# Softmax denominators of a transformer block: five of sixteen tiles a head summed by accumulating DMA

## The chip, the core and the metric

The kernel runs on one core of a Trainium2 chip. The metric is the device time of one execution in microseconds (us). The engines are PE (TensorE), DVE (VectorE), ACT (ScalarE), POOL (GpSimd) and SP (SyncE, which here only issues DMAs). Each runs its own instructions in order and waits for the others by semaphores. The core has 16 DMA engines; a DMA can be issued by SP, ACT or POOL.

## The reference, cut to what matters

A transformer block with adaptive norms: B=2 sequences, L=2048 rows, D=512, H=16 heads of 32, a hidden width of 1024.

```
shift_msa, scale_msa, gate_msa, shift_mlp, scale_mlp, gate_mlp = split(silu(c) @ Wada + bada, 6)
h = _ln(x) * (1 + scale_msa) + shift_msa
q, k, v = h @ Wq + bq, h @ Wk + bk, h @ Wv + bv        # 16 heads each
A = softmax(q @ k.T / sqrt(32))                         # 2048 x 2048 for each of 32 (batch, head) pairs
x = x + gate_msa * ((A @ v) @ Wo + bo)
h2 = _ln(x) * (1 + scale_mlp) + shift_mlp
out = x + gate_mlp * (gelu(h2 @ W1 + b1) @ W2 + b2)
```

## The kernel before, in words

Three stages follow one another. The first computes the modulation, the norm and q, k, v in eight chunks of 512 rows. The second is attention: 32 heads (`g`, G = 32), each in 16 steps (`t`, NT = 16), one step for each tile of 128 keys against all 2048 queries. The third projects, and runs the MLP in eight chunks. Large products are made of a rounded high part and a low remainder ("hi" and "lo"), three matmuls for one.

In step `t` of head `g` PE computes the scores of tile `t` in four parts of 512 queries (L1338, L1340, L1342 and the subtraction of the row maximum, L1347), 16 matmuls; between them four "maximum" matmuls (L1326) of the next head, which DVE reduces (L1055); then `values`, the product of v with the exponentials of tile `t-1` (L1360). ACT turns each score bank into exponentials (L844), four to a tile, in `prob`, a ring of RING = 4 tiles: the exponentials of tile `t` overwrite those of tile `t-4`, so ACT waits first until the last reader of tile `t-4` is done (in `probs`).

The denominator of the softmax is the sum of the exponentials over all 2048 keys. It is collected in two ways. Tiles 0, 1, 3, 4, 6, 7, 9, 10, 12 and 13 (POOL_TILES) are added up by POOL in `psum_acc`, in halves of 1024 columns, nine adds a head and half (`sum_probs`, L695). Their sum, and each of the tiles 2, 5, 8, 11, 14 and 15 (PE_TILES), are summed over the partitions by a group of four matmuls with ones (`sums_of`, L1351), each tile's group one step after its scores, the group of POOL's sum at step 1 of the next head. ACT copies each group's bank (L822) and issues a DMA of the row to DRAM (L824). SP reads the 7 rows of a head back (`load_sums`), DVE adds them and takes the reciprocal at step 8 of the next head (`denominators`).

POOL may start a head's adds only when the group over its last sum is done (`den_mm`), since `psum_acc` is used again.

Seven PSUM banks are given out by a table made in advance (`bank_table`), which takes for each use the bank that should be free first; PE waits in `bank_free` for the former user of that bank, an exponential, a maximum or a copy of sums. The table decides which wait stands where.

The weights wo and w1 (12 pieces of 128 x 512, `late`) are loaded and split during heads 0 to 5, two pieces a head, at steps 4 and 11: ACT writes the high part (L804), DVE the low part (`split_late_lo`, L1087) between its maximum reduces.

`gate` and `gate_b` hold the two gates on all partitions; `gate` is written in the first stage and next read in head 31 (`residual1`, L1115).

## Time and profile before

| what | us |
|---|---|
| median of 3 runs | 2526.02 (2525.95 to 2527.97) |
| the profiled execution | 2520.45 |
| its span in the trace | 2518.7 |
| PE busy | 2405.8 (96%) |
| DVE busy | 1757.6 (70%) |
| POOL busy | 1506.6 (60%) |
| ACT busy | 1421.9 (56%) |

The profiled execution is one run of its own; what lies around its span is 1.75 us. The attention stage runs from about 360 us to about 2050 us. Busy shares are means over three stages with different limits, so the part of the attention that repeats (from 732 us on) is read by itself. In the rows below a line number such as L1351 is the line of the kernel above, an idle time in square brackets stands before the first instruction of its row and names what ended it, and a row with x8 merges eight instructions.

### The profile page before, as it was taken

Reading aid. Unit: us, or ns where it says so; the run is one execution under the profiler, and the core shown is the slowest. Engines: PE = TensorE matmul, PEld = TensorE weight load, DVE = VectorE, ACT = ScalarE, POOL = GpSimd, SP = SyncE. Lnnn points to the kernel's source line nnn. Section 1 sums busy time; section 2 is a strip of 40 time slices with the busy share of each in tenths; the row PEclk is TensorE's granted clock in tenths of the full one; section 3 lists DMA queues with packets and bytes.
Section 4 is the critical chain, followed back from the end, with each engine's and each line's share of the span. In section 5 each row is a group of like instructions: output and inputs, shape, how many; then the busy total and the mean of one; then the engine's idle time right before and its main releaser. Section 6 shows DMA issues by size and latency. Waiting matters only on the chain.

```text
span 2518.7 us, 49885 instructions
## 1 busy us (share of the span) xinstructions
PE 2405.8 (96%) x19544; PEld 1356.3 (54%) x19544; DVE 1757.6 (70%) x2878; ACT 1421.9 (56%) x2622; POOL 1506.6 (60%) x706
## 2 busy tenths in 40 slices
PE   7999889988899999999999999999999888999998
PEld 5788653433344444444444444444444347888887
DVE  5444567777778888888888888888888326566563
ACT  3233225666677777777777777777777542222221
POOL 0000116777688788878887888888788634332320
PEclk9999988999999999999999999999999889999999
DMA  8655561332222332233223322332332111332200
GB/s 273 212 172 187 150 172 35 76 69 62 62 54 54 79 80 54 58 75 80 54 60 79 75 54 67 80 66 54 79 80 50 49 57 50 101 82 67 67 34 34
DMA packets 212631, 210.39 MB, mean 84 GB/s; under 512 B 120064, under 2 KB 152832, under 8 KB 203008
## 3 DMA queue, kind: packets, MB, share of 16 engines
q1 hardware_dynamic: 209904, 205.59, 31.5%
q8 instruction: 143, 2.34, 0.4%
q10 hardware_dynamic: 2512, 1.86, 0.3%
q14 instruction: 72, 0.59, 0.1%
HBM read 146.30 MB, written 60.82 MB: 82 GB/s over the span
## 4 chain that ended last, share of the span: by engine, by line
PE 86%; DVE 4%; ACT 3%; DMA 2%; issue 2%; POOL 1%; SPq 1%; ACTq 0%; POOLq 0%
PE ps L1360 19%; PE ps L1229 19%; PE ps L1326 10%; PE ps L1338 9%; PE ps L1351 8%; PE ps L1469 7%; PE ps L1340 6%; PE ps L1342 4%; PE ps L1347 3%; ACT work L844 1%; DVE weights_r L1087 1%; DVE part_max L1055 1%; POOL work L695 1%; PE ps L1238 1%; ACT work L822 1%
## 5 line engine op out<-in xcount | busy, mean ns | idle before, releaser
L695 POOL TENSOR_TENSOR work<-work 128x1024 f32<-128x1024 f32 x576 | 1355.1, 2409 | 384.7 <-PE ps L1351 227.2
L1055 DVE TENSOR_REDUCE part_max<-ps 128x1 f32<-128x512 f32 x1984 | 1232.1, 682 | 306.6 <-PE ps L1326 306.6
L844 ACT ACTIVATE work<-ps 128x512 f32<-128x512 f32 x2048 | 1058.9, 602 | 382.0 <-PE ps L1347 355.8
L1360 PE MATMUL ps<-work 128*32 128x512 f32 x4096 | 556.8, 616 | 0.2 <-ACT work L844 0.2
L1326 PE MATMUL ps<-acts_r 32*128 32x512 f32 x1344 | 420.5, 478 | 26.1 <-DVE part_max L1055 23.9
L1229 PE MATMUL ps<-acts_r,weights_r 128*128 128x512 f32 x1536 | 381.9, 399 | 4.9 <-DVE acts_r L975 3.9
L1229 PEld LDWEIGHTS ps<-acts_r,weights_r 128*128 128x128 f32 x1536 | 292.2, 192 | 69.8 <-issue 6.8
L1338 PEld LDWEIGHTS ps<-acts_r 32*128 32x128 f32 x1408 | 146.5, 186 | 323.2 <-DVE part_max L1055 172.4
L1338 PE MATMUL ps<-acts_r 32*128 32x512 f32 x1408 | 299.5, 474 | 16.5 <-ACT work L844 7.9
L1340 PE MATMUL ps<-acts_r 32*128 32x512 f32 x1408 | 259.3, 398 | 0.0
L1326 PEld LDWEIGHTS ps<-acts_r 32*128 32x128 f32 x1344 | 182.0, 185 | 137.7 <-DVE part_max L1055 121.7
L1351 PE MATMUL ps<-work,ones 128*32 128x512 f32 x1792 | 242.1, 613 | 0.0
L1347 PE MATMUL ps<-acts_r,minus_r 1*128 1x512 f32 x1024 | 230.6, 446 | 0.2 <-DMA acts_r<-max_T 0.2
L1347 PE MATMUL ps<-m_odd,minus_r 1*128 1x512 f32 x1024 | 228.2, 442 | 0.0
L897 ACT ACTIVATE work<-ps,b_sb 128x512 f32<-128x512 f32 x64 | 44.0, 690 | 307.7 <-PE ps L1229 307.7
L1326 PE MATMUL ps<-acts_r,w_r 32*128 32x512 f32 x640 | 200.7, 474 | 14.2 <-DVE part_max L1055 13.2
L1229 PE MATMUL ps<-weights_r,acts_r 128*128 128x512 f32 x768 | 186.2, 396 | 12.4 <-DVE acts_r L1105 9.4
L668 POOL TENSOR_TENSOR var_eps<-var_eps,mv 128x4 f32<-128x4 f32 x16 | 3.2, 203 | 316.1 <-DVE mv L953 316.1
L710 POOL TENSOR_TENSOR work<-work,gate_b 128x512 f32<-128x512 f32 x60 | 86.1, 1467 | 169.8 <-DMA work<-in_x 149.4
L1342 PE MATMUL ps<-acts_r 32*128 32x512 f32 x1024 | 186.3, 397 | 0.0
L1342 PE MATMUL ps<-w_r,acts_r 32*128 32x512 f32 x1024 | 185.5, 396 | 0.0
L1469 PE MATMUL ps<-w_r,acts_r 128*128 128x512 f32 x768 | 184.4, 391 | 0.0
(88 smaller groups left out, 2553.7 us busy)
## 6 DMA issues: line engine op xcount, KB each, us to landing
acts_r<-k_hi SPq DMA_DIRECT2D x130, 256.0 KB, 4.7
acts_r<-k_lo SPq DMA_DIRECT2D x129, 256.0 KB, 4.8
work<-in_x SPq DMA_DIRECT2D x16, 1024.0 KB, 5.3
q_hi<-work SPq DMA_DIRECT2D x32, 256.0 KB, 2.6
q_lo<-work SPq DMA_DIRECT2D x32, 256.0 KB, 3.3
k_hi<-work SPq DMA_DIRECT2D x32, 256.0 KB, 2.5
k_lo<-work SPq DMA_DIRECT2D x32, 256.0 KB, 3.2
v_rows<-work SPq DMA_DIRECT2D x32, 256.0 KB, 2.0
```

The lines of the kernel that those rows point to most:

```text
L695: nc.gpsimd.tensor_tensor(psum_acc[:, at], first, prob[:, t % RING, at], ALU.add).then_inc(add_ok, 1)
L844: nc.scalar.activation(prob[:, t % RING, j * CH:(j + 1) * CH], ps[:, bank, :], ACT.Exp, scale=SCALE).then_inc(exp_ok, 1)
L1055: nc.vector.tensor_reduce(part_max[:, r * TT + q // NQ, q % NQ:q % NQ + 1], ps[:, bank, :], AX.X, ALU.max).then_inc(a_max, 1)
L1229: mm = nc.tensor.matmul(o, lhs(s, kk), rhs(r, kk), start=(kk == 0 and s == r), stop=(kk == KC - 1 and s == 1))
L1326: nc.tensor.matmul(ps[:, use[0], :], q_hi[u][at, q // NQ * P:(q // NQ + 1) * P], k_hi[u][at, q % NQ * CH:(q % NQ + 1) * CH], start=True, s ...
L1338: nc.tensor.matmul(o, k_hi[u][at, keys], q_hi[u][at, :], start=True, stop=False)
L1340: nc.tensor.matmul(o, k_lo[w][at, keys], q_hi[u][at, :], start=False, stop=False)
L1342: nc.tensor.matmul(o, k_hi[u][at, keys], q_lo[w][at, :], start=False, stop=False)
L1347: nc.tensor.matmul(o, minus_r[row, :], m_row[w][row, :], start=False, stop=True).then_inc(b_mm, 1)
L1351: mm = nc.tensor.matmul(ps[j * DH:(j + 1) * DH, bank, :], ones[:, 0:DH], src(j), start=True, stop=True)
L1360: mm = nc.tensor.matmul(ps[j * DH:(j + 1) * DH, O_BANK, :], v_sb[g % TWO][:, t, :], prob[:, t % RING, j * CH:(j + 1) * CH], start=(t == 0) ...
L1469: mm = nc.tensor.matmul(ps[:, 4 + t, :], g_r[:, f % 4, s, t * P:(t + 1) * P], w2_r[:, r, f, :], start=(f == 0 and s == r), stop=(f == FB - ...
```

## The change

DMA_TILES = 2, 5, 8, 11, 13 are no longer summed by PE or (13) by POOL. When the exponentials of such a tile are there, POOL issues a DMA of the whole tile, 128 partitions x 2048 columns (1 MB), from `prob` to `rest_acc`: the first of a head writes, the four others add to what is there (`accum_op`). `rest_acc` is the memory of `gate`; `gate` is stored in DRAM in the first stage and loaded again in head 31. POOL waits for the landing of each such DMA before it issues the next, ACT waits for it before it overwrites the ring slot, and the first DMA of a head waits until PE's group over the former head's `rest_acc` is done. That group stands at step 3 of the next head. POOL adds nine tiles (eight adds), PE has groups for tiles 14 and 15, POOL's sum and `rest_acc`: 4 groups a head in place of 7. Head 31 has no such DMA; its groups are 8 in place of 7.

The low parts of the late weight pieces are made by POOL at the start of heads 1 to 12, one piece a head, and ACT makes the high part at step 11 of heads 0 to 11. SP loads one piece a head.

The diff, cut to its core:

```diff
-POOL_TILES = [0, 1, 3, 4, 6, 7, 9, 10, 12, 13]
-PE_TILES = [t for t in range(NT) if t not in POOL_TILES]
+POOL_TILES = [0, 1, 3, 4, 6, 7, 9, 10, 12]
+DMA_TILES = [2, 5, 8, 11, 13]
 NADD = len(POOL_TILES) - 1
-ND = len(PE_TILES) + 1
+NDMA = len(DMA_TILES)
+REST_STEP = 3
...
+def pe_tiles(g):
+
+    return [t for t in range(NT) if t not in POOL_TILES and (g == G - 1 or t not in DMA_TILES)]
+
+
+def groups_of(g):
+
+    return len(pe_tiles(g)) + (1 if g == G - 1 else 2)
+
+
+ND = groups_of(0)
+ND_MOST = groups_of(G - 1)
...
-            tiles = [(t - 1) % NT] if (g or t) and (t - 1) % NT in PE_TILES else []
-            groups = [PE_TILES.index(tile) for tile in tiles] + ([ND - 1] if g and t == 1 else [])
-            for n, d in enumerate(groups):
-                uses["sums"].append((d, *use("D", now + until["D"] + 2 * n, range(2, 3) if tail else banks)))
+            owner = g if t else g - 1
+            groups = [(owner, pe_tiles(owner).index((t - 1) % NT))] if owner >= 0 and (t - 1) % NT in pe_tiles(owner) else []
+            if g and t == 1:
+                groups.append((g - 1, len(pe_tiles(g - 1))))
+            if g and t == REST_STEP:
+                groups.append((g - 1, ND - 1))
+            for n, (o, d) in enumerate(groups):
+                uses["sums"].append((o, d, *use("D", now + until["D"] + 2 * n, range(2, 3) if tail else banks)))
...
+        rest_acc = gate[:].rearrange("p w b d -> p (w b d)")
...
-        LATE_STEPS = (4, 11)
-        LATE_HEADS = len(late) // len(LATE_STEPS)
+        LATE_STEP = 11
...
+            sp.wait_ge(gateb_ok, 2 * B)
+            sp.dma_start(gate_dram, gate[0:1, :, :, :]).then_inc(gate_out, 16)
...
+            sp.wait_ge(rest_mm, G - 1)
+            sp.dma_start(rest_acc, gate_dram.broadcast_to((P, 2 * B * D))).then_inc(gate_in, 16)
...
-                for k in range(NADD):
-                    t = POOL_TILES[k + 1]
+                for t in range(POOL_TILES[1], NT):
                     if t in between:
                         between[t]()
-                    for h in range(HALVES):
-                        pool.wait_ge(exp_ok, START + g * FILLS + t * NQ + (h + 1) * NQ // HALVES)
-                        at = slice(h * L // HALVES, (h + 1) * L // HALVES)
-                        if k:
-                            pool.wait_ge(add_ok, START + (g * NADD + k - 1) * HALVES + h + 1)
-                        first = prob[:, POOL_TILES[0] % RING, at] if k == 0 else psum_acc[:, at]
-                        nc.gpsimd.tensor_tensor(psum_acc[:, at], first, prob[:, t % RING, at], ALU.add).then_inc(add_ok, 1)
+                    if t in POOL_TILES:
+                        k = POOL_TILES.index(t) - 1
+                        for h in range(HALVES):
+                            pool.wait_ge(exp_ok, START + g * FILLS + t * NQ + (h + 1) * NQ // HALVES)
+                            at = slice(h * L // HALVES, (h + 1) * L // HALVES)
+                            if k:
+                                pool.wait_ge(add_ok, START + (g * NADD + k - 1) * HALVES + h + 1)
+                            first = prob[:, POOL_TILES[0] % RING, at] if k == 0 else psum_acc[:, at]
+                            nc.gpsimd.tensor_tensor(psum_acc[:, at], first, prob[:, t % RING, at], ALU.add).then_inc(add_ok, 1)
+                    elif t in DMA_TILES and g < G - 1:
+                        n = g * NDMA + DMA_TILES.index(t)
+                        pool.wait_ge(exp_ok, START + g * FILLS + (t + 1) * NQ)
+                        if n:
+                            pool.wait_ge(rest_in, 16 * n)
+                        if t == DMA_TILES[0]:
+                            if g:
+                                pool.wait_ge(rest_mm, g)
+                            else:
+                                pool.wait_ge(gate_out, 16)
+                            pool.dma_start(rest_acc, prob[:, t % RING, :]).then_inc(rest_in, 16)
+                        else:
+                            pool.dma_start(rest_acc, prob[:, t % RING, :], accum_op=ALU.add).then_inc(rest_in, 16)
...
+            def split_late_lo(k):
+                pool.wait_ge(late_hi, k + 1)
+                hi, lo = late[k][1]
+                nc.gpsimd.tensor_tensor(lo, tmp3[:, k % 2, :], hi.bitcast(F32), ALU.subtract).then_inc(late_lo, 1)
 
             for g in range(G - 1):
+                if 0 < g <= len(late):
+                    split_late_lo(g - 1)
...
+                        elif last in DMA_TILES and gl < G - 1:
+                            act.wait_ge(rest_in, 16 * (gl * NDMA + DMA_TILES.index(last) + 1))
...
-            def split_late_lo(k):
-                dve.wait_ge(late_hi, k + 1)
-                hi, lo = late[k][1]
-                nc.vector.tensor_tensor(lo, tmp3[:, k % 2, :], hi.bitcast(F32), ALU.subtract).then_inc(late_lo, 1)
-
-
             for g in range(G - 1):
-                first = g * len(LATE_STEPS)
-                head(g, {t: lambda k=first + i: split_late_lo(k) for i, t in enumerate(LATE_STEPS) if g < LATE_HEADS})
+                head(g)
...
+                if isinstance(n, int) and n == 0:
+                    dve.wait_ge(gate_in, 16)
...
+                        pe.wait_ge(rest_in, 16 * (g + 1) * NDMA)
+                        sums_of(lambda j: rest_acc[:, j * CH:(j + 1) * CH], use[0]).then_inc(rest_mm, 1)
```

The order on POOL at the start of the attention and over head 0 of before (L679 splits a part of w2, L695 is the add of half a tile; the later heads have the same 18 rows without `w2_lo`):

```order
L679 TENSOR_TENSOR w_r<-work,w_r 128x2048 [waits w_hi]
L679 TENSOR_TENSOR w_r<-work,w_r 128x1536 [waits w_hi]
L695 TENSOR_TENSOR work<-work 128x1024 [waits exp_ok,den_mm,w2_lo]
L695 TENSOR_TENSOR work<-work 128x1024 [waits exp_ok]
L695 TENSOR_TENSOR work<-work 128x1024 [waits add_ok,exp_ok] x16
```

And over one head (1 to 12) of the changed kernel, from the low part of a weight piece (L746) on (L728 is the add, L739 the writing DMA, L741 the adding one):

```order
L746 TENSOR_TENSOR weights_r<-tmp,weights_r 128x512 [waits late_hi]
L728 TENSOR_TENSOR work<-work 128x1024 [waits exp_ok,den_mm]
L728 TENSOR_TENSOR work<-work 128x1024 [waits exp_ok]
L739 DMA gate<-work 128x2048 [waits rest_mm,rest_in,exp_ok]
L728 TENSOR_TENSOR work<-work 128x1024 [waits add_ok,exp_ok] x4
L741 DMA gate<-work 128x2048 [waits rest_in,exp_ok]
L728 TENSOR_TENSOR work<-work 128x1024 [waits add_ok,exp_ok] x4
L741 DMA gate<-work 128x2048 [waits rest_in,exp_ok]
L728 TENSOR_TENSOR work<-work 128x1024 [waits add_ok,exp_ok] x4
L741 DMA gate<-work 128x2048 [waits rest_in,exp_ok]
L728 TENSOR_TENSOR work<-work 128x1024 [waits add_ok,exp_ok] x2
L741 DMA gate<-work 128x2048 [waits rest_in,exp_ok]
```

Two halves (one tile) fewer are added, five DMAs stand between the adds, and each waits for the one before it.

On PE, the end of step 6 of head 3 of before, and the start of the next (the group L1351 over tile 5):

```order
L1347 MATMUL ps<-m_odd,minus_r 128x512 x2
L1360 MATMUL ps<-work 32x512 [waits exp_ok]
L1360 MATMUL ps<-work 32x512 x3
L1351 MATMUL ps<-work,ones 32x512 [waits exp_ok]
L1351 MATMUL ps<-work,ones 32x512 x3
L1338 MATMUL ps<-acts_r 128x512 [waits a_max]
```

The same place in the changed kernel (L1411 is `values`, L1389 the first score matmul, L1377 the maximum matmul):

```order
L1398 MATMUL ps<-m_odd,minus_r 128x512 x2
L1411 MATMUL ps<-work 32x512 [waits exp_ok]
L1411 MATMUL ps<-work 32x512 x3
L1389 MATMUL ps<-acts_r 128x512 [waits exp_ok]
L1389 MATMUL ps<-acts_r 128x512 [waits a_max]
L1377 MATMUL ps<-acts_r 128x512 [waits exp_ok]
```

The group is gone, and the first score matmul of the next step waits for an exponential (`exp_ok`) where it waited for a maximum (`a_max`).

## Rows read from the trace of the kernel before

**Rows 1.** The page's part 1 (busy time, share, instructions) and part 4 (chain).
```profile
PE 2405.8 (96%) x19544; PEld 1356.3 (54%) x19544; DVE 1757.6 (70%) x2878; ACT 1421.9 (56%) x2622; POOL 1506.6 (60%) x706
...
PE 86%; DVE 4%; ACT 3%; DMA 2%; issue 2%; POOL 1%; SPq 1%; ACTq 0%; POOLq 0%
```

**Rows 2.** Stretches: length, busy time of PE, PEld, DVE, ACT, POOL; clock; DMA share, GB/s.
```profile
435.52:732.74 297.22, 265.07 (x2524) 116.63 (x2527) 229.37 (x350) 194.24 (x371) 214.71 (x90) 0.93 0.27 64
732.74:1031.11 298.37, 297.76 (x3028) 133.93 (x3030) 243.60 (x408) 225.76 (x433) 253.16 (x109) 1.00 0.31 68
1031.11:1080.81 49.70, 49.60 (x508) 22.35 (x509) 40.60 (x68) 37.63 (x73) 42.19 (x19) 1.00 0.30 67
```

**Rows 3.** Timeline of PE: start, duration, instruction; L1338 opens a step.
```profile
1008.45 0.50 PE L1338 MATMUL ps<-w_r,acts_r 32*128 32x512 f32 x2
...
1011.17 0.50 PE L1338 MATMUL ps<-w_r,acts_r 32*128 32x512 f32 x2
...
1014.76 0.50 PE L1338 MATMUL ps<-w_r,acts_r 32*128 32x512 f32 x2
...
1030.92 0.50 PE L1338 MATMUL ps<-acts_r 32*128 32x512 f32 x2
...
1037.22 0.49 PE L1338 MATMUL ps<-acts_r 32*128 32x512 f32 x2
```

**Rows 4.** Timeline of POOL over one head.
```profile
1031.11 4.73 POOL L695 TENSOR_TENSOR work<-work 128x1024 f32<-128x1024 f32 x2 [7.25 <-PE ps L1351]
1036.09 37.46 POOL L695 TENSOR_TENSOR work<-work 128x1024 f32<-128x1024 f32 x16 [0.26 <-ACT work L844]
1080.81 4.73 POOL L695 TENSOR_TENSOR work<-work 128x1024 f32<-128x1024 f32 x2 [7.25 <-PE ps L1351]
```

**Rows 5.** Timeline of ACT at the exponentials of tile 4.
```profile
1037.98 0.48 ACTq L824 DMA_DIRECT2D partial_sums<-work  x1
1038.59 2.07 ACT L844 ACTIVATE work<-ps 128x512 f32<-128x512 f32 x4 [0.64 <-POOL work L695]
```

**Rows 6.** DVE's L1087 (duration ns min/median/max), and a subtraction of its size with POOL idle.
```profile
L1087 DVE TENSOR_TENSOR weights_r<-tmp,weights_r x12: 1470/2463/4344, 379.0 to 709.8; 128x512 fp32r<-128x512 f32 x12
...
2015.60 0.69 DVE L1157 TENSOR_TENSOR w_r<-work,w_r 128x512 fp32r<-128x512 f32 x1 [16.70 <-ACT w_r L869]
```

**Rows 7.** Timeline of PE around a gap, and the stretch behind it.
```profile
470.66 0.39 PE L1326 MATMUL ps<-acts_r,w_r 32*128 32x512 f32 x1
473.50 0.49 PE L1326 MATMUL ps<-acts_r,w_r 32*128 32x512 f32 x1 [2.45 <-DVE part_max L1055]
...
473.93 1.67 PE L1360 MATMUL ps<-work 128*32 128x512 f32 x8
475.35 1.95 PE L1351 MATMUL ps<-work,ones 128*32 128x512 f32 x8
477.24 0.68 PE L1338 MATMUL ps<-acts_r 32*128 32x512 f32 x2
...
473.00:476.00 3.00, 2.50 (x15) 0.71 0.00 0
```

**Rows 8.** DMA issues: queue, count, KB each, median us from issue to landing.
```profile
work<-in_x SPq DMA_DIRECT2D x16, 1024.0 KB, 5.3
...
out_y<-work SPq DMA_DIRECT2D x7, 1024.0 KB, 4.3
...
gate_b<-in_wada SPq DMA_DIRECT2D x1, 1024.0 KB, 9.7
...
out_y<-work SPq DMA_DIRECT2D x4, 256.0 KB, 2.0
```

**Rows 9.** POOL's 128x512 instruction in the third stage (busy, mean ns).
```profile
L710 POOL TENSOR_TENSOR work<-work,gate_b 128x512 f32<-128x512 f32 x60 | 86.1, 1467 | 169.8 <-DMA work<-in_x 149.4
```

**Rows 10.** Timeline of DVE in head 31: the first read of the gate.
```profile
2016.21 0.68 DVE L1115 TENSOR_TENSOR tmp<-ps,gate 128x512 f32<-128x512 f32 x1
```

More of the change, by code:

```diff
@@ L107, in bank_table @@
         heads.append(steps)
-    end = [(d, *use("D", now, range(2, 3))) for d in (PE_TILES.index(NT - 1), ND - 1)]
+    end = [(G - 1, d, *use("D", now, range(2, 3))) for d in (ND_MOST - 2, ND_MOST - 1)]
     return heads, end
 USES, USES_END = bank_table()
-assert NT - 1 in PE_TILES
+assert NT - 1 in pe_tiles(0)
+LAST_SUM = [max(use[4] for steps in [*USES, [{"sums": USES_END}]] for uses in steps for use in uses["sums"] if use[0] == g)
+            for g in range(G)]
 def block_kernel(nc, x, cT, wq, wk, wv, wo, w1, w2, wada, bqT, bkT, b1T, badaT, bada, bv, bo, b2, out):
@@ L317, in block_kernel @@
                         *v_out, *o_out]
-        SUMS_END = USES[G - 1][0]["sums"][0][3]
+        SUMS_END = USES[G - 1][0]["sums"][0][4]
         def sums_buffer(n):
@@ L521, in store_rec, with load_late @@
                 sp.dma_start(rec_dram[g:g + 1, :].rearrange("o (p x) -> (o p) x", x=NT), rec_c[:]).then_inc(rec_out, 16)
-            def load_late(g):
-                for k in range(g * len(LATE_STEPS), (g + 1) * len(LATE_STEPS)):
-                    if k >= 2:
-                        sp.wait_ge(late_hi, k - 1)
-                        sp.wait_ge(late_lo, k - 1)
-                    sp.dma_start(tmp3[:, k % 2, :], late[k][0]).then_inc(late_in[k % 2], 16)
+            def load_late(k):
+                if k >= 2:
+                    sp.wait_ge(late_hi, k - 1)
+                    sp.wait_ge(late_lo, k - 1)
+                sp.dma_start(tmp3[:, k % 2, :], late[k][0]).then_inc(late_in[k % 2], 16)
             def head(g):
@@ L542, in head @@
                 store_head(g - 1, (g - 1) % TWO)
-                if g + 1 < LATE_HEADS:
+                if g + 1 < len(late):
                     load_late(g + 1)
@@ L846, in probs @@
                         take_output(g - 1)
-                    take_sums(g if t > 1 else g - 1, USES[g][t]["sums"])
+                    take_sums(USES[g][t]["sums"])
                     if t in between:
@@ L851, in late_pieces @@
             def late_pieces(g):
-                first = g * len(LATE_STEPS)
-                return {t: lambda k=first + i: split_late_hi(k) for i, t in enumerate(LATE_STEPS) if g < LATE_HEADS}
+                return {LATE_STEP: lambda: split_late_hi(g)} if g < len(late) else {}
             probs(0, late_pieces(0))
@@ L884, in _ @@
             take_output(G - 1)
[L885 removed]
+            take_sums(USES_END[1:])
             def stage3(c, b, nxt):
@@ L1407, in head @@
                         values(g - 1, NT - 1)
-                    take_sums(g if t > 1 else g - 1, uses["sums"])
+                    take_sums(uses["sums"])
                     if t in between:
@@ L1438, in first_projection @@
                 if t == 0:
-                    pe.wait_ge(sums_ok, USES[G - 1][1]["sums"][-1][3])
+                    pe.wait_ge(sums_ok, USES[G - 1][1]["sums"][-1][4])
                     pe.wait_ge(late_lo, len(late))
```

52 lines of the change are left out of this document (30 added, 22 removed).

## The prediction

> **What bounds the kernel now.** I read the page's busy shares and chain first: PE is busy 96% of the span and is 86% of the chain [rows 1]. That is a mean over three stages, so the next view is the stretches of the attention. Over six heads from 732.74 to 1031.11 us, and over one head from 1031.11 to 1080.81, PE is busy 99.8% at clock 1.00, DVE 82%, ACT 76%, POOL 85% [rows 2]. A steady head takes 49.70 us and PE sets it. The five heads 1 to 5, 435.52 to 732.74 us, take 297.22 us, PE busy 89%, clock 0.93 [rows 2]: there it is held up.
>
> Next, the steps on PE. A plain one takes 2.72 us (1008.45 to 1011.17), one with a group of sums 3.59 (1011.17 to 1014.76), so a group costs 0.87 us [rows 3]. Sixteen plain steps and seven groups make 43.5 + 6.1 = 49.6, the head as measured.
>
> Last, POOL's timeline, since the change gives it new work. It begins 7.25 us after its former head's end, when PE's group over its sum is done at 1030.9, has 4.73 us for the first tile, and 37.46 for the eight others, 4.68 a tile with nearly no gap [rows 4]. Step 4 begins at 1037.22 [rows 3], and the exponentials of its tile start at 1038.59, 1.37 us later, 2.07 us for four; there ACT even waits for POOL last [rows 5]. So POOL has few microseconds to spare, and through the ring of four tiles a late POOL is a late ACT.
>
> **The change, part by part.**
>
> Groups removed. Heads 0 to 30 have four groups in place of seven. If PE went on setting the pace, a steady head would take 49.70 - 3 x 0.87 = 47.1 us. Head 31 has one group more, +0.9 us. The four groups stand at steps 15, 0, 1 and 3; step 2 and steps 4 to 14 are plain. I call S4 the start of step 4; from step 0 of the next head to its S4 there are three steps with a group and one plain, 13.5 us.
>
> Late pieces. On DVE a low part takes 1.47 to 4.34 us, median 2.46, beside POOL's adds; a subtraction of that size takes 0.69 when POOL is idle [rows 6]. PE stands still for it and comes back at a lower clock (below). Five steady heads would take 5 x 49.73 = 248.6 us; they take 297.2, so ten pieces cost 48.6, 4.9 each, and with the two of head 0 about 58. On POOL a 128x512 instruction takes 1.47 us [rows 9], and it lies in the 7.25 us in which POOL waits at the head's start [rows 4]: nothing. ACT's high part stays. If POOL's idle time were gone, 12 x 1.47 = 18 us would come back. I take -58.
>
> The DMAs. The trace shows no DMA issued by POOL and none that adds. Two prices are unknown: i, the time POOL is held by one issue, and L, from POOL's being ready to the landing. For i the nearest rows are ACT's issue, 0.48 us [rows 5], and a POOL instruction, 1.47 [rows 9]; I take 0.8, between them and nearer the issue. For L the rows give 4.3 us for 1 MB out of the same kind of buffer and 2.0 for 256 KB, so 0.77 for each 256 KB and 1.2 fixed; 5.3 for a 1 MB load; 9.7 for one that shares the engines with others [rows 8]. An adding DMA has to read what it adds to, so 2 MB are read: 1.2 + 8 x 0.77 = 7.4. Bounds: 4.3 and 9.7. I take 7.4.
>
> What these do to a head. At S4 the group over the former `rest_acc` is done, and POOL may issue tile 2's DMA. From there POOL is a chain: i; tiles 3 and 4 (9.4 us); i (tile 5); 6 and 7; i (tile 8); 9 and 10; i (tile 11). Tile 11's DMA starts at S4 + 28.2 + 3i and lands L later, and only then may ACT write tile 15. By before's spacing those exponentials would start 11 plain steps and 1.37 us after S4, at 31.3. With i = 0.8 and L = 7.4 they start at 28.2 + 2.4 + 7.4 = 38.0. PE can't run ahead of that: the next step's first banks are those of the first two exponentials, so the next step starts about 1.1 us after the exponentials do (two take 1.04 of the 2.07). Then 13.5 us to the next S4. The head therefore is at least
>
> 28.2 + 3i + L + 1.1 + 13.5 = 42.8 + 3i + L = 52.6 us.
>
> The other DMAs close shorter or equal loops: tile 8's gives 42.4 + 2i + L = 51.4, and tile 13's, which must wait for tile 11's landing, 35.6 + 3i + 2L = 52.8 (28.2 + 3i + 2L, 1.1, and two steps, 6.3). Even with the DMA landing at once, POOL's add of tile 10 before tile 14 gives 46.3 + 3i = 48.7.
>
> What the gap costs beyond itself. PE stood 2.45 us at 471, and after it one value and one group row took from 473.93 to 477.24, 3.31 us in place of about 1.8, with granted clock 0.71 (between its levels 1.2 and 2.4 GHz) [rows 7]. A gap of 2 to 3 us so costs about 1.5 more. Tile 9 would wait 2.5 us for tile 5's DMA, tile 12 under 1 (PE being slow after the first gap), tile 15 2.3, and the steps behind that lie on the loop: +1.5. The head is 54.1 us, 4.4 more than before. Thirty heads (1 to 30) close this loop; head 0 is longer anyway. 30 x 4.4 = +132.
>
> The gates. The store in the first stage is 8 KB. The reload is behind the group at step 3 of head 31, one more 1 MB load on SP's queue, 5.3 us; the gate is first read at 2016.21 [rows 10], some 20 us after that: nothing, at most 5 if it lies before the last weight piece's load. SP's load of the sums now waits for step 3 in place of 1, and behind it stand the next head's loads of low parts, needed a whole head later: nothing.
>
> Sum, against the profiled execution: 2520.45 - 58 + 132 + 1 = 2595. The median of the runs lies 5.6 us above it, so 2601 for the median, 3.0% slower; the times below are set against the median too.
>
> On L the Trainium skill speaks ("DMA: Bandwidth & Descriptors", Anatomy of one DMA): for a DMA issued by GpSimd it gives about 2.0 us plus the bytes over 436 GB/s, 4.4 us for 1 MB. No run here shows it yet; it counts a plain copy, and the same page's rules for kernel authors say that an accumulate reads its destination and writes it later, which speaks for the double reading. It also gives GpSimd's first byte about 1 us where SP's and ACT's have 0.6 (Specifications). By 4.4 and i = 1 the loop would be 50.2 us and the sum an estimated 2484 us, the side of the first rival below.
>
> **The rivals.**
>
> The landing is short. If the second reading is overlapped and the DMA behaves as the 1 MB load does, L = 5.3, and the issue costs as on ACT, i = 0.48: 42.8 + 1.4 + 5.3 = 49.5, no gap long enough for the clock; 30 x (49.5 - 49.7) = -6, with -57 for the rest: 2463. For it: the removed groups are real PE time and the pieces' 58 us come whatever the DMAs do; the DMA engines are used 30% in a steady head. Against it: three streams in place of two. Its best end, i = 0.48 and L = 4.3, is 48.5 a head, 2433. This case decides as soon as 3i + L is under 7.4 with the clock's term or 8.8 without it: there the sum is 0. With the landing hidden altogether a head would be 47.1 and the time 2391, but 46.3 + 3i already excludes that.
>
> The queue is crowded. SP's loads take 30% of the DMA engines [rows 2], in bursts, and five DMAs of 1 MB, reading two each, come between. With L = 9.7 and i = 1 tile 13's loop sets the head: 35.6 + 3 + 19.4 + 1.5 = 59.5, 30 x 9.8 = +294, 2763. For it: the 9.7 us row. Against it: that load ran beside several of 1 MB each.
>
> Loss and gain cancel where the head is 51.6 us: POOL's chain then takes back the groups and the pieces too. Nothing in the rows speaks for just this value.
>
> **How the numbers follow.** What a measurement here can tell from no change is 0.2%, 5 us. The forecast (landing sets the head, slower) has chance 0.52, with 2550 to 2660 as its own range; the short landing 0.32; the crowded queue 0.12; the cancelling case 0.04. So slower 0.64, faster 0.32, same 0.04. The range runs from 2437, near the best end of the short landing, to 2710, where tile 13's loop with L = 9 ends: 35.6 + 2.7 + 18 + 1.5 = 57.8, 30 x 8.1 - 57 = +186.
>
> **What would show it.** Right: in the stretches of a steady head PE busy falls to about 88%, the head is 54 us, ACT waits for the `rest_acc` DMAs some 5 us a head, 160 in all, with PE's clock under 1.00; the DMAs' row shows landing near 7 us; heads 1 to 5 are as long as the later ones, and DVE has no row on weights. Wrong: a landing under 6 us, an issue under 0.5, or ACT's wait for the DMAs near zero; and on the other side a landing over 9. If heads 1 to 5 are still longer than the later ones, the pieces' term was wrong.

## The result and the profile after

The changed kernel takes 2682.3 us in the median of four runs (2681.14 to 2687.01), beside 2526.44 (2525.95 to 2527.97) for the kernel before: 1.062 times as long, 95% interval 1.060 to 1.064. It is 156 us slower. The forecast was 75 us slower, so the change cost twice what it said.

The page of the kernel after answers [rows 1] with these lines:

```profile
PE 2411.9 (90%) x18808; PEld 1354.8 (51%) x18808; DVE 1726.0 (64%) x2866; ACT 1365.1 (51%) x2530; POOL 1491.6 (56%) x809
...
PE 53%; DMA 29%; issue 8%; ACT 4%; POOL 4%; DVE 2%; SPq 1%; ACTq 0%; POOLq 0%
```

PE fell from 86% of the chain to 53%, and DMA rose from 2% to 29%. The stretches say the same, head by head (columns as in [rows 2], which they answer: several of heads 1 to 5, and one steady head):

```profile
428.00:732.00 304.00, 270.70 (x2568) 120.44 (x2564) 216.48 (x365) 193.74 (x374) 227.71 (x118) 0.91 0.69 154
...
1003.38:1059.06 55.68, 50.80 (x488) 22.58 (x484) 40.58 (x69) 36.35 (x71) 42.79 (x23) 0.91 0.70 154
```

A steady head takes 55.7 us here, and 57.27 in the mean over 29 heads (1 to 29, from 430.16 us to 2091.04, each from its first DMA to that of the next), where it was 49.7. PE is busy 91% of it and the granted clock is 0.91, where both were 1.00. The DMA share went from 0.30 to 0.70. In heads 1 to 5 the clock and PE's share are now those of the later heads: the late pieces no longer disturb.

POOL's timeline over that steady head answers [rows 4]. Line 739 is the first DMA of a head (tile 2), line 741 the adding ones (tiles 5, 8, 11, 13):

```profile
1003.38 0.59 POOL L739 DMA_DIRECT2D gate<-work  x1 [2.41 <-PE ps L1402]
1003.99 9.38 POOL L728 TENSOR_TENSOR work<-work 128x1024 f32<-128x1024 f32 x4
1013.32 0.86 POOL L741 DMA_DIRECT2D gate<-work  x1
1013.93 9.56 POOL L728 TENSOR_TENSOR work<-work 128x1024 f32<-128x1024 f32 x4
1023.19 1.14 POOL L741 DMA_DIRECT2D gate<-work  x1
1023.80 9.87 POOL L728 TENSOR_TENSOR work<-work 128x1024 f32<-128x1024 f32 x4
1033.09 1.43 POOL L741 DMA_DIRECT2D gate<-work  x1
1034.24 5.01 POOL L728 TENSOR_TENSOR work<-work 128x1024 f32<-128x1024 f32 x2
1042.02 0.88 POOL L741 DMA_DIRECT2D gate<-work  x1 [2.77 <-DMA gate<-work]
1042.63 1.60 POOL L746 TENSOR_TENSOR weights_r<-tmp,weights_r 128x512 fp32r<-128x512 f32 x1
1052.24 4.73 POOL L728 TENSOR_TENSOR work<-work 128x1024 f32<-128x1024 f32 x2 [8.01 <-PE ps L1402]
1059.06 0.60 POOL L739 DMA_DIRECT2D gate<-work  x1 [2.09 <-PE ps L1402]
```

From tile 2's DMA to tile 11's at 1033.09 POOL never waits for a landing in this head. Tile 13's DMA can't follow until tile 11's has landed, at 1041.5. The low weight part (L746) lies in the idle time behind that, as forecast, 1.60 us. The chain of waits in the same head shows what the landings do to the end:

```profile
1033.09 8.39 DMA gate<-work
1041.52 0.50 issue
1042.02 8.32 DMA gate<-work
1050.41 0.61 ACT work L901
```

Two landings stand one behind the other, 8.39 and 8.32 us, with 0.50 between. ACT (L901 is the exponentials) waits for three of the five DMAs in this head:

```profile
1022.28 2.06 ACT L901 ACTIVATE work<-ps 128x512 f32<-128x512 f32 x4 [5.33 <-DMA gate<-work]
...
1050.41 2.07 ACT L901 ACTIVATE work<-ps 128x512 f32<-128x512 f32 x4 [1.95 <-DMA gate<-work]
```

These are tile 9 (overwrites tile 5) and the next head's tile 1 (over 13); between them tile 15 (over 11) waits 0.8. Over the whole trace the view of waits gives, with the total, the count and the longest:

```profile
ACT work L901 <- DMA gate<-work: 283.9, 80, 6.8
```

That wait did not exist before. Last, PE alone in four pieces of the head (length, PE busy, clock, DMA share, GB/s), and from 700 to 1950 us the row of the adding DMAs and the landings of all DMAs into `gate`, the plain one of tile 2 with them:

```profile
1003.38:1022.90 19.52, 15.78 (x164) 0.96 0.81 191
1022.90:1031.80 8.90, 8.87 (x60) 0.52 0.59 120
1031.80:1043.70 11.90, 11.89 (x128) 1.00 0.60 124
1043.70:1059.06 15.36, 14.26 (x152) 1.00 0.70 148
```

```profile
L741 POOL DMA_DIRECT2D gate<-work x86: 850/885/1482, 728.3 to 1940.8; - x86
...
DMA to landing us min/median/max: 4.6/7.9/11.4
```

Before 1022.90 PE had stood 3.8 us behind the exponentials of tile 9; then it ran 8.9 us at a granted clock of 0.52, the 1.2 GHz level.

The landings differ by tile. Means over the 31 heads with DMAs, from issue to landing, read issue by issue in the trace: tile 2 (plain) 5.0, tile 5 9.4, tile 8 7.5, tile 11 7.9, tile 13 9.3 us.

### The profile page after: what moved, and what is told of

Same layout as the page of the kernel before. It is cut to its first block, busy times and chain, and to the rows that moved or that the text cites. A ratio compares the mean times of both kernels' runs of the same rounds, so it can differ in the third digit from the quotient of the medians.

```text
span 2679.8 us, 48354 instructions
## 1 busy us (share of the span) xinstructions
PE 2411.9 (90%) x18808; PEld 1354.8 (51%) x18808; DVE 1726.0 (64%) x2866; ACT 1365.1 (51%) x2530; POOL 1491.6 (56%) x809
## 3 DMA queue, kind: packets, MB, share of 16 engines
q0 software_dynamic: 22320, 162.54, 27.8%
## 4 chain that ended last, share of the span: by engine, by line
PE 53%; DMA 29%; issue 8%; ACT 4%; POOL 4%; DVE 2%; SPq 1%; ACTq 0%; POOLq 0%
DMA gate<-work 27%; PE ps L1280 18%; PE ps L1411 8%; PE ps L1523 6%; PE ps L1389 6%; POOL work L728 3%; PE ps L1377 3%; ACT work L901 3%; PE ps L1391 3%; PE ps L1402 3%; PE ps L1393 2%; PE ps L1398 1%; PE ps L1289 1%; DMA acts_r<-k_hi 1%; DVE part_max L1111 1%
## 5 line engine op out<-in xcount | busy, mean ns | idle before, releaser
L728 POOL TENSOR_TENSOR work<-work 128x1024 f32<-128x1024 f32 x512 | 1234.1, 2589 | 399.9 <-PE ps L1402 300.9
L901 ACT ACTIVATE work<-ps 128x512 f32<-128x512 f32 x2048 | 1057.8, 602 | 661.1 <-PE ps L1398 374.6
L1411 PE MATMUL ps<-work 128*32 128x512 f32 x4096 | 583.5, 644 | 0.1
L1377 PE MATMUL ps<-acts_r 32*128 32x512 f32 x1344 | 428.1, 504 | 3.1 <-DVE part_max L1111 1.3
L1389 PE MATMUL ps<-acts_r 32*128 32x512 f32 x1408 | 324.0, 501 | 96.6 <-ACT work L901 87.5
L1389 PEld LDWEIGHTS ps<-acts_r 32*128 32x128 f32 x1408 | 159.6, 197 | 435.6 <-ACT work L901 287.4
L1391 PE MATMUL ps<-acts_r 32*128 32x512 f32 x1408 | 280.3, 423 | 0.0
L1377 PEld LDWEIGHTS ps<-acts_r 32*128 32x128 f32 x1344 | 191.1, 197 | 107.3 <-DVE part_max L1111 81.7
L1398 PE MATMUL ps<-m_odd,minus_r 1*128 1x512 f32 x1024 | 233.6, 459 | 0.0
L1377 PE MATMUL ps<-acts_r,w_r 32*128 32x512 f32 x640 | 204.1, 499 | 0.8
L1393 PE MATMUL ps<-w_r,acts_r 32*128 32x512 f32 x1024 | 203.2, 422 | 0.0
L1393 PE MATMUL ps<-acts_r 32*128 32x512 f32 x1024 | 201.7, 422 | 0.0
L1389 PE MATMUL ps<-w_r,acts_r 32*128 32x512 f32 x640 | 146.5, 502 | 43.2 <-ACT work L901 43.2
```

The costliest lines, as they stand in the source:

```text
L728: nc.gpsimd.tensor_tensor(psum_acc[:, at], first, prob[:, t % RING, at], ALU.add).then_inc(add_ok, 1)
L901: nc.scalar.activation(prob[:, t % RING, j * CH:(j + 1) * CH], ps[:, bank, :], ACT.Exp, scale=SCALE).then_inc(exp_ok, 1)
L1377: nc.tensor.matmul(ps[:, use[0], :], q_hi[u][at, q // NQ * P:(q // NQ + 1) * P], k_hi[u][at, q % NQ * CH:(q % NQ + 1) * CH], start=True, s ...
L1389: nc.tensor.matmul(o, k_hi[u][at, keys], q_hi[u][at, :], start=True, stop=False)
L1391: nc.tensor.matmul(o, k_lo[w][at, keys], q_hi[u][at, :], start=False, stop=False)
L1393: nc.tensor.matmul(o, k_hi[u][at, keys], q_lo[w][at, :], start=False, stop=False)
```

## The experiments

Theory A is the forecast's: the landing of the adding DMAs closes the loop through the ring of four tiles. What each experiment adds to it stands beside it. "Head" is the mean of the steady heads, from POOL's first DMA of one to that of the next.

| kernel | median us | ratio to before (95%) | head | landings by tile |
|---|---|---|---|---|
| late pieces only | 2467.95 | 0.977 (0.976 to 0.979) | | |
| no DMA | 2383.6 | 0.944 (0.942 to 0.947) | | |
| plain DMAs | 2540.93 | 1.006 (1.005 to 1.008) | 52.3 | 4.9, 7.4, 4.8, 4.9, 5.8 |
| half a tile added | 2546.18 | 1.008 (1.005 to 1.012) | 52.4 | 5.1, 6.7, 5.0, 5.7, 6.8 |
| the change | 2682.3 | 1.062 (1.060 to 1.064) | 57.3 | 5.0, 9.4, 7.5, 7.9, 9.3 |
| low loads left out | 2721.49 | 1.080 (1.075 to 1.085) | 58.5 | 5.1, 7.5, 7.6, 8.3, 9.9 |
| without tile 5 | 2697.03 | 1.069 (1.067 to 1.072) | 57.6 | 5.3, -, 7.5, 8.1, 9.6 |
| without tile 13 | 2620.59 | 1.038 (1.036 to 1.039) | 55.2 | 5.2, 9.4, 7.5, 7.8, - |
| earlier issue | 2726.24 | 1.079 (1.078 to 1.081) | 58.8 | 5.1, 11.1, 7.5, 7.6, 8.1 |

### Each half of the change alone

The late pieces alone, on the kernel before:

```diff
-        LATE_STEPS = (4, 11)
+        LATE_STEP = 11
...
             for g in range(G - 1):
+                if 0 < g <= len(late):
+                    split_late_lo(g - 1)      # on POOL; DVE's is gone
```

> Only the weight pieces are changed: low part on GpSimd at the start of heads 1 to 12, one piece a head, no DMA by GpSimd, ten tiles added by GpSimd and six summed by PE as before. Theory A (the pieces on VectorE cost heads 0 to 5 about 4.9 us each, 58 in all, and GpSimd's wait at a head's start hides them): heads 1 to 5 are 49.7 us, 2468 us in all. Rival (those heads are long for another reason, the pieces being only in the way): heads 1 to 5 stay near 59 us, 2515 to 2526.

2467.95 against 2525.71: -57.8, the forecast's -58 to the microsecond. The stretch from 425 us, which holds five heads, is undisturbed:

```profile
425.00:700.00 275.00, 274.46 (x2794) 123.50 (x2788) 224.10 (x375) 211.41 (x406) 237.98 (x104) 1.00 0.34 76
```

The other half with its DMAs and all waits on them left out:

```diff
-                            pool.dma_start(rest_acc, prob[:, t % RING, :]).then_inc(rest_in, 16)
...
-                            pool.dma_start(rest_acc, prob[:, t % RING, :], accum_op=ALU.add).then_inc(rest_in, 16)
...
-                        elif last in DMA_TILES and gl < G - 1:
-                            act.wait_ge(rest_in, 16 * (gl * NDMA + DMA_TILES.index(last) + 1))
```

> The changed kernel without the five DMAs a head and the waits for their landing (tiles 2, 5, 8, 11 and 13 are left out of the denominators in heads 0 to 30; PE still sums the gate's memory at step 3, and GpSimd still waits for that group). Theory A: the head is PE's 47.1 us or GpSimd's chain of adds, 0.7 + 46.3 = 47.0: 47.1, some 2390 us in all. Theory C (the bank table): the head is 50 us or more, over 2475.

2383.6, with PE busy all the time at full clock:

```profile
900.00:1500.00 600.00, 598.89 (x6104) 277.47 (x6101) 514.49 (x868) 455.63 (x878) 483.06 (x208) 1.00 0.32 69
```

The new bank table and order of groups so cost nothing, and the groups left out are worth 84 us behind the 58 of the pieces. Everything lost, 299 us from here to the changed kernel, is the DMAs'.

### What of the DMA costs

The same DMAs, but copying where they added:

```diff
-pool.dma_start(rest_acc, prob[:, t % RING, :], accum_op=ALU.add).then_inc(rest_in, 16)
+pool.dma_start(rest_acc, prob[:, t % RING, :]).then_inc(rest_in, 16)
```

> The changed kernel with all five DMAs of a head as plain writes (the sum over the tiles is left out, so the denominators are not the reference's); queue, waits and bytes from the source are the same. Theory A (the ring is closed by the landing of the adding DMA, 8.4 to 9 us where the plain one takes 4.7): landing 4.7, tile 11's loop is 0.7 + 28.2 + 3 x 0.6 + 4.7 + 0.3 + 1.1 + 13.5 = 50.3 us a head, some 2480 us in all. Theory B (GpSimd's software queue, the issues and their place behind the adds, cost the time): head 54 us or more, over 2590. Theory C (without the groups PE is tied closer to ScalarE by the bank table, whatever the DMAs do): head over 54 us too, with ScalarE's waits for DMAs near zero.

2540.93 lies between the two numbers: I had taken every plain landing at the quick value, and tile 5's was not quick (below). The row of the queue has the same packets and bytes but 17.2% of the engines' time; with four of the five adding it is 27.8%. The first two lines are of this kernel's page, the other two of the changed one's:

```profile
q0 software_dynamic: 22320, 162.54, 17.2%
...
gate<-work POOLq DMA_DIRECT2D x155, 1024.0 KB, 4.9
```

```profile
q0 software_dynamic: 22320, 162.54, 27.8%
...
gate<-work POOLq DMA_DIRECT2D x155, 1024.0 KB, 8.0
```

A plain landing has a median of 4.9 us, which agrees with the 4.4 us that the forecast took from the Trainium skill ("DMA: Bandwidth & Descriptors", Anatomy of one DMA) to half a microsecond; the adding one takes 8.0. But tile 5's copy took 7.4, and ACT's row shows the wait that it made:

```profile
1020.45 2.06 ACT L901 ACTIVATE work<-ps 128x512 f32<-128x512 f32 x4 [3.17 <-DMA gate<-work]
```

That is not the adding. This wait sets the head of the plain kernel: in 27 of its 29 steady heads PE is idle for less than 0.3 us from tile 5's landing (1.2 us behind it) to the next head's first DMA. From tile 2's DMA to tile 5's are 9.9 us, the landing takes 7.45, and then come ten steps on PE, four of them with a group (30.7 us by [rows 3]), with 0.65 before them and 0.7 behind. That makes 49.4; 52.3 is measured, and PE's clock is 0.92 from the landing on. So the forecast's list of loops lacked one, tile 5's.

In the changed kernel tile 5's DMA goes out at 1013.32 and tile 13's at 1042.02, and SP's queue in that kernel has, just before the one and beside the other:

```profile
1006.48 3.12 SPq L510 DMA_DIRECT2D w_r<-q_lo  x4
1009.64 1.81 SPq L506 DMA_DIRECT2D acts_r<-k_lo  x4
1011.49 0.43 SPq L518 DMA_DIRECT2D work<-v_rows  x1
...
1042.69 3.99 SPq L510 DMA_DIRECT2D w_r<-q_hi  x4
1046.72 3.45 SPq L506 DMA_DIRECT2D acts_r<-k_hi  x4
```

The loads of q are 64 KB each, those of k and v 256 KB. So two of five DMAs run beside SP's loads. The Trainium skill has the rule in the same page (Issuing engines are not separate DMA queues): DMAs of all issuers run on the same 16 DMA engines and interleave. The trace agrees. For tile 5 it gives the size: 7.4 beside 4.9 plain, 9.4 beside 7.5 adding, and without those loads the adding one took 7.5 (next part). For tile 13 and the high parts it is less sure, since no kernel left those loads out: 5.8 beside 4.9 plain and 9.2 beside 7.9 adding, tile 11's being the other number.

Half of each tile added, the first still copied whole:

```diff
-pool.dma_start(rest_acc, prob[:, t % RING, :], accum_op=ALU.add).then_inc(rest_in, 16)
+pool.dma_start(rest_acc[:, 0:L // 2], prob[:, t % RING, 0:L // 2], accum_op=ALU.add).then_inc(rest_in, 16)
```

> The changed kernel with the four adding DMAs of a head on half a tile (1024 of 2048 columns; the other half of tiles 5, 8, 11 and 13 is left out of the denominators). Theory A (the landing is set by the bytes moved, the adding ones being read twice): a landing of 4.5 to 5 us as for a plain DMA of 1 MB, the head near 52 us as with plain DMAs, 2520 to 2550 in all. Rival E (adding has a fixed cost, whatever the size): landing over 6.5, head over 55, over 2620.

2546.18, as a plain DMA of twice the bytes. The landings fell to 5.0 (tile 8) from 7.5: the cost of adding goes with the bytes. An adding 512 KB lands as late as a plain 1 MB, which fits the forecast's double reading; no row shows the reads themselves.

### Which loop sets the head

The tile 9 gap was the largest, 5.33 us on ACT. If it were what costs, taking the collision away from tile 5 should win. The low parts' loads were left out from the third head on:

```diff
-                sp.wait_ge(pv_mm, START + g * NT)
-                load_lo(g + 1, (g + 1) % TWO)
-                load_v(g + 1, (g + 1) % TWO)
```

> The changed kernel without SP's loads of the low parts of k and q and of v for heads 2 to 31 (those heads use what heads 0 and 1 left). In the changed kernel tile 5's DMA lands after 9.4 us on average, tile 8's after 7.5, tile 11's after 7.9, tile 13's after 9.3; the low loads are issued 3 to 8 us after tile 2's DMA, just ahead of tile 5's. Theory A2 (these loads share the DMA engines with tile 5's DMA and cost it 2 us, and the longer gap lowers PE's clock): tile 5's landing falls to about 7.5, ScalarE's wait there from 5.3 us to under 4, the head from 57.3 to 54.5 to 55.5, 2610 to 2640 in all. Rival D (an adding DMA's landing does not depend on SP's loads): 2675 to 2690, landings as they are.

Tile 5's landing fell from 9.4 to 7.5 as it should if the loads were the cause, and yet the kernel was slower, 2721.49. Both theories had the time wrong. ACT's rows at tiles 9, 15 and 1:

```profile
1031.74 2.06 ACT L898 ACTIVATE work<-ps 128x512 f32<-128x512 f32 x4 [3.41 <-DMA gate<-work]
...
1053.17 2.07 ACT L898 ACTIVATE work<-ps 128x512 f32<-128x512 f32 x4 [3.52 <-DMA gate<-work]
...
1062.92 2.06 ACT L898 ACTIVATE work<-ps 128x512 f32<-128x512 f32 x4 [2.13 <-DMA gate<-work]
```

The time that tile 9 no longer waited was waited at tile 15. Tile 5's landing is on a loop that is too short to count here: POOL has 28 us of adds of its own between the group at S4 and tile 11's DMA, and goes through them nearly whether ACT stands or not (30.0 us with its issues in the mean, 29.7 where it never waits). The head closes over POOL's adds, tile 11's landing, tile 13's landing and the way back to S4. In the changed kernel PE has no idle time from tile 13's landing (1.2 us behind it) to the next head's first DMA, in none of the 29 heads; behind tile 5's landing it still has 2.1 us a head. By the trace of this kernel against the changed one, in means over 29 heads: from tile 2's DMA to tile 11's 29.7 for 30.0, tile 11's landing 8.4 for 7.9, tile 13's 9.95 for 9.2, from there to the next tile 2's DMA 9.9 for 9.5. Together that is the 1.2 us more. Why tiles 11 and 13 land later without those loads was not settled.

So theory A3: tile 13's loop. Two kernels tell it from rival G, that tile 5's gap with its clock sets the time. Tile 5 back to PE:

```diff
-DMA_TILES = [2, 5, 8, 11, 13]
+DMA_TILES = [2, 8, 11, 13]
```

> The changed kernel with tile 5 summed by PE again (DMAs for tiles 2, 8, 11, 13; five groups a head). In the changed kernel ScalarE waits longest for tile 5's DMA, 5.3 us beyond its usual pause in the head looked at, and PE's clock is 0.52 for 9 us behind it. Theory A3 (the head is set by the chain from tile 2's issue over GpSimd's adds to tile 11's landing and tile 13's landing behind it; the gap at tile 5 only fills time that would be waited later): the head loses one issue, 0.6, and keeps the rest, 56 to 57 us, 2635 to 2675 in all. Rival G (the gap at tile 5 and the low clock after it are what the head pays): the head falls by 5 or more, to 52, under 2560.

2697.03: G is out. It is above A3's range too: the head is a little longer than the changed kernel's, 57.6. The issue did come back, 29.2 us from tile 2's DMA to tile 11's in place of 30.0. It was given away again: tile 11's landing 0.15 longer, tile 13's 0.5, the way back 0.5. Why these landings are longer is open, as before. The gap only stands elsewhere, in this trace at tile 12's exponentials, which wait for tile 8's DMA:

```profile
1054.86 2.06 ACT L901 ACTIVATE work<-ps 128x512 f32<-128x512 f32 x4 [4.59 <-DMA gate<-work]
```

Tile 13 back to PE:

```diff
-DMA_TILES = [2, 5, 8, 11, 13]
+DMA_TILES = [2, 5, 8, 11]
```

> The changed kernel with tile 13 summed by PE (DMAs for tiles 2, 5, 8, 11; five groups a head). Theory A3: the second landing of 9.3 us leaves the chain, tile 11's loop is left: 0.7 + 28.2 + 1.8 + 7.9 + 0.5 + 1.1 + 13.5 + 0.9 = 54.6 us, and up to 1.5 more if the gap at tile 15 now lowers the clock: 54.5 to 56, 2600 to 2645 in all. Rival G: no change, 2675 to 2690, since the longest gap stays.

2620.59, in A3's range: the same number of DMAs as the one before, 76 us less. That tile 13's double landing sets the changed kernel's head stands by this pair. What is left is not tile 11's loop, though, as A3 had it. With the measured terms that one is 42.8 + 3 x 0.6 + 7.8 + 0.7 + 0.55 = 53.7 (0.7 us pass from S4 to tile 2's DMA, and PE's next step starts 1.65 us behind the landing in place of 1.1, see below), and 55.2 is measured. The 1.5 that the forecast had for the clock can't fill this, since behind tile 11's landing the granted clock is 1.00 in all 29 heads. Tile 5's loop fills it. ACT waits for landings 40 times in the trace, about once a head. In the head at 1039 us it is at tile 9:

```profile
1058.50 2.07 ACT L901 ACTIVATE work<-ps 128x512 f32<-128x512 f32 x4 [5.92 <-DMA gate<-work]
```

From 1.2 us behind that landing to the next head's first DMA PE is idle for 0.1 us at most in each of the 29 heads, at a mean clock of 0.91. The terms are those of the plain kernel with one group more: 9.9 to tile 5's DMA, 9.4 for its landing, 0.65 + 31.6 + 0.7 for the steps, 52.3, and 3 us for the low clock behind the gap. The same terms give the changed kernel's tile 5 loop 54.3 us, 3 under its 57.3. So A3's number came true by another loop than the one it named.

### POOL's queue

If landing sets the head, an earlier issue should help. POOL's order was written out so that each DMA goes as soon as its tile is there (D is a DMA, .0 and .1 are halves of an add):

```diff
+POOL_ORDER = '1 D2 3 D5 4 6.0 D8 6.1 7 D11 9 10 D13 12'.split()
...
+                for item in POOL_ORDER:
+                    if item[0] == "D":
+                        send(int(item[1:]))
```

> The changed kernel with GpSimd's order changed: each adding DMA is issued as soon as its tile is there, ahead of adds that can wait (order 1, D2, 3, D5, 4, first half of 6, D8, second half of 6, 7, D11, 9, 10, D13, 12). Same DMAs, same adds. Theory A (the landing is late because the issue is late): every landing comes by the natural start of the exponentials or within 1 us, and the add of tile 10 behind four issues sets the head: 0.7 + 28.2 + 4 x 0.6 + 1.1 + 3.6 + 13.5 = 49.5 us, 2455 to 2490 in all. Theory B2 (what counts is how many bytes the DMA engines move, the landings just take longer when put earlier beside the loads of the next head): head over 54 us, over 2600.

2726.24: my number fell, the rival's holds. POOL stood before DMAs, and ACT, which had waited 0.6 us for POOL's adds in the whole attention, waited 300:

```profile
1038.15 0.88 POOL L742 DMA_DIRECT2D gate<-work  x1 [3.50 <-DMA gate<-work]
```

```profile
ACT work L911 <- POOL work L726: 300.2, 117, 4.8
```

A DMA put ahead of adds in an in-order queue makes the adds wait for what the DMA waits for: its tile and the former landing. 38 us of adds in a head of 50 leave no room for that.

### Fewer DMAs

The rows point to DMAs that stand far apart, none behind another, and away from SP's loads. Four kernels tried this. All keep ten tiles for POOL where the DMAs are two or three, as the kernel before does. Tiles 2 and 14:

```diff
-POOL_TILES = [0, 1, 3, 4, 6, 7, 9, 10, 12]
-DMA_TILES = [2, 5, 8, 11, 13]
+POOL_TILES = [0, 1, 3, 4, 6, 7, 9, 10, 12, 13]
+DMA_TILES = [2, 14]
+POOL_ORDER = '1 D2 3 4 6 7 9 10 12.0 D14 12.1 13'.split()
```

> Two tiles a head by DMA, those whose slots are needed latest relative to the queue: tile 2 (plain) and tile 14 (adding, issued between the halves of tile 12's add); ten tiles added by GpSimd as before, PE sums 5, 8, 11 and 15; the weight pieces on GpSimd. The slot of tile 14 is needed at step 2 of the next head, three steps with a group later. Theory A: PE sets the head, 49.7 - 0.87 = 48.8 us, 2468 - 26 = 2442. Rival F (GpSimd, which does ten tiles and two issues, becomes late for the ring or for its sum): head over 49.7, over 2468.

2460.98 (ratio 0.973, 0.972 to 0.975), head 49.6, between the two numbers. Tiles 2, 5 and 14, with D5 behind the add of 3:

```diff
+DMA_TILES = [2, 5, 14]
+POOL_ORDER = '1 D2 3 D5 4 6 7 9 10 12.0 D14 12.1 13'.split()
```

> As the version with tiles 2 and 14, with tile 5 by DMA as well, issued before the add of tile 4: PE sums 8, 11 and 15. Theory A with A2: tile 5's DMA, beside SP's low loads, lands after 10 to 11 us, 1 to 2 us later than its slot is wanted, and GpSimd's chain is late by what it waits: head 49 to 50.5 us, 2450 to 2490, no better than with two tiles. If the landing is hidden: 47.9 us, 2416.

2528.33 (1.001, 0.999 to 1.002), above the range: 67 us more than without tile 5. Its DMA landed after 11.0 us, beside SP's low loads, as expected. In the head at 1004 us POOL did not stand for it: the eleven adds behind its issue run without a pause. ACT did, 4.62 us in that head and 107.6 for landings over the whole trace, where it was 3.8 without tile 5.

Tiles 2 and 14 again, the rest's group at step 2 and D14 later:

```diff
+REST_STEP = 2
+POOL_ORDER = '1 D2 3 4 6 7 9 10 12 13.0 D14 13.1'.split()
```

> The version with tiles 2 and 14 by DMA again, with what its trace shows to be late mended: the group over rest_acc at step 2 in place of 3, so that tile 2's DMA is issued 2.7 us earlier (ScalarE waited 1.5 us for it), and tile 14's DMA between the halves of tile 13's add in place of tile 12's (GpSimd waited 1.9 us for the exponentials of tile 14 there, and ScalarE then for GpSimd). Theory A: PE sets the head, 48.8 us, 2440 to 2448 in all. Rival H (ScalarE or the bank table ties the head at 49.6 whatever is mended): 2458 to 2464.

2466.26 (0.976, 0.974 to 0.977), head 49.7: no gain over the former, both numbers missed. By [rows 3] a head of 16 plain steps and six groups is 43.5 + 6 x 0.87 = 48.7. Of the missing microsecond 0.9 stands in the two steps behind the rest's group, 3.40 and 2.98 us in place of 2.72 in the head at 1009 us, and much the same in the five heads behind it. Just before them ACT waits for tile 14's DMA, which now goes out later and lands after 9.5 us:

```profile
1026.54 2.06 ACT L911 ACTIVATE work<-ps 128x512 f32<-128x512 f32 x4 [1.25 <-DMA gate<-work]
```

Over the trace ACT's wait for landings is 36.7 us here, 3.8 in the former. By these rows the later issue of tile 14's DMA cost what the earlier group was to save; no run undid it alone.

Tiles 2, 8 and 14, with the same ten for POOL:

```diff
+DMA_TILES = [2, 8, 14]
+REST_STEP = 2
+POOL_ORDER = '1 D2 3 4 6 7.0 D8 7.1 9 10 12 D14 13'.split()
```

> As the mended version with tiles 2 and 14, and tile 8 by DMA too, issued between the halves of tile 7's add, well after SP's low loads; PE sums 5, 11 and 15. Theory A with A2 (away from SP's loads an adding DMA lands in 7.5 us, just in time for tile 12; tile 14's in 8.8): 47.9 to 48.5 us a head, 2416 to 2435. If the landings come 1 to 2 us late after all, gaps and GpSimd's waits bring it to 50 us, 2475 or more.

2426.23 us (2422.97 to 2428.75; ratio 0.960, 0.959 to 0.962), in the range expected: 99 us under the kernel before and 42 under the late pieces alone. It does the whole computation and is faster than both. POOL's timeline over a head:

```profile
1011.91 0.59 POOL L740 DMA_DIRECT2D gate<-work  x1
1013.93 16.39 POOL L726 TENSOR_TENSOR work<-work 128x1024 f32<-128x1024 f32 x7 [1.43 <-ACT work L911]
1030.26 0.82 POOL L742 DMA_DIRECT2D gate<-work  x1
1030.88 16.58 POOL L726 TENSOR_TENSOR work<-work 128x1024 f32<-128x1024 f32 x7
1047.22 1.08 POOL L742 DMA_DIRECT2D gate<-work  x1
```

The DMAs are 13 to 18 us apart, so each has landed (5.2, 7.5 and 9.1 us) well before the next, and none has a wait before it. ACT waits for them 16.5 us in all. PE keeps its clock:

```profile
900.00:1500.00 600.00, 595.78 (x6042) 269.75 (x6036) 501.46 (x839) 451.09 (x869) 548.59 (x262) 1.00 0.60 135
```

## Why the prediction was right and wrong

**What bounded the kernel before**: PE in a steady head, with POOL nearly full. Right: with the DMAs gone PE is busy 99.8% and the time falls by 142 us.

**The late pieces, -58.** Right, -57.8 measured alone.

**The groups.** Right: 47.1 a head and 2391 us with the landing hidden; 2384 measured without DMAs.

**The issue, i = 0.8.** 0.6: POOL's next instruction starts 0.6 us behind four of the five issues in the rows above, plain or adding (the issue's row of 0.86 to 1.43 overlaps the add's). Behind tile 11's it starts after 1.15, where tile 12's exponentials are only just there.

**The gates.** Right. The reload is issued at 2154.24 and the gate first read at 2177.01, 22.8 us later; nothing waits.

**The loop.** Its mechanism was right: an adding landing closes the ring, ACT waits for it (the forecast said some 5 us a head and 160 in all; 284 was measured), PE's clock drops. The step that failed is the landing L = 7.4, taken for all DMAs alike, and with it the choice of tile 11's loop, 52.6, over tile 13's, 52.8, the only one that holds two landings (and by the forecast's own numbers the longer). Tile 13's is the one that sets the head; its second landing takes 9.2 us, and the hand-overs between its parts were put at nothing and take 1.25. For tile 5 the forecast wrote down no loop; it is the next one, and sets the head as soon as tile 13's is gone. Its terms, from S4 to S4, forecast and measured in means over 29 heads of the changed kernel:

| term | forecast | measured |
|---|---|---|
| S4 to tile 2's DMA | 0 | 0.7 |
| from there to tile 11's DMA | 28.2 + 2.4 | 30.0 |
| tile 11's landing | 7.4 | 7.9 |
| until tile 13's DMA goes out | 0 | 0.55 |
| tile 13's landing | 7.4 | 9.2 |
| to the next step on PE and two steps, to S4 | 1.1 + 6.3 | 8.8 |
| head | 52.8 | 57.2 |

Of the 4.4 us, 2.3 are the landings, 1.8 of them tile 13's, which runs beside the loads of k_hi and q_hi. 1.25 are two hand-overs that the forecast took at nothing. 1.4 is the way back, and it has two parts. In the head shown PE's next step starts 1.65 us behind the landing (1050.41 to 1052.06) where 1.1 was forecast: PE waits for the first exponentials, and then the group of step 1 (1051.06) comes before the next step. The other 0.9 is the clock. From tile 13's landing to the next head's first DMA 15 of the 29 heads take 8.67 to 8.75 us at a granted clock of 1.00, and the other 14 take 9.85 to 11.35 at 0.69 to 0.83. The shorter issue gave 0.6 back. The forecast's own head was 54.1, with 1.5 for the clock on its loop; against that the clock cost less, 0.9, and the landings and hand-overs are all the more what it lacked.

The forecast had 7.4 for a landing alone and that size was right: tile 8's, beside no such load, takes 7.5. In part that was luck. The same 1.2 + 0.77 for each 256 KB gives 4.3 for a plain 1 MB and for an adding 512 KB, and those take 4.9 and 5.0. From 5.0 and 7.5 I estimate 2.5 fixed and 0.63 for each 256 KB; the two errors cancel at 2 MB. Wrong was to put the collision with SP's loads into a rival as one condition for all five DMAs. It had to be asked for each DMA at its place in the head, and SP's loads were there to see. The second rival ("the queue is crowded") named the right loop, and its price, 59.5 a head with L = 9.7 and i = 1, was too high because tile 11's DMA runs free (7.9) and an issue holds POOL 0.6.

**The clock's price.** PE's timeline of the changed kernel, at the starts of steps 10, 11 and 12:

```profile
1022.93 0.79 PE L1389 MATMUL ps<-w_r,acts_r 32*128 32x512 f32 x2 [3.76 <-ACT work L901]
...
1027.78 0.79 PE L1389 MATMUL ps<-w_r,acts_r 32*128 32x512 f32 x2
...
1031.77 0.50 PE L1389 MATMUL ps<-w_r,acts_r 32*128 32x512 f32 x2
```

After a gap of 3.76 us two steps took 8.84 us in place of 5.44, at the granted clock of 0.52 seen above. That is +3.4, where I had 1.5 from a gap of 2.45 us [rows 7]. In this kernel it cost little, since this gap lies beside POOL's 28 us, on a loop 3 us shorter than tile 13's.

**The sum.** Thirty heads by 7.54 us (57.27 - 49.73) are +226 in place of +132. With -58 that is +168; the profiled execution, 2681.61 us, is +161. Of the 7 us between them head 0 gives 4: it got 13.5 us shorter, where the pieces' share is 9.8. The rest I did not account for. The time lies above the forecast's own range (2550 to 2660) and inside the wide one.

By kernels, from 2526: -58 for the pieces, -84 for the groups, +157 for five 1 MB copies with their waits (tile 5's loop sets 27 of 29 heads there), +141 for the adding.

## What to carry to other kernels

When work moves to DMAs that hand buffers back, write for each of them the loop from one fixed point of an iteration to the same point of the next, and sum every landing that stands in it one behind another: two serial landings a head cost here what no single wait row shows. The longest wait of the head shown (5.33 us at tile 9) was on a shorter loop, and shortening its DMA gained nothing; but it set the head once the longer loop was gone. Before calling what is left by the name of a loop, look where PE is idle behind its landing. Price each landing at its own place in the iteration, against what other queues move there. Space such DMAs wider than their slowest landing, and put one ahead of work in an in-order queue only where that work can afford to wait for what the DMA waits for.
